# Copying the carries of two states in one GpSimd operation, with four scan buffers, a ring of two channel pairs for dt*x, and a new table of places

## What is computed

```python
x, z = split(hidden @ in_proj_w.T)                  # 1024 channels each
x = silu(causal_conv(x, conv_w, taps=4) + conv_b)
dt, Bm, Cm = split(x @ x_proj_w.T)                  # 64, 16, 16 columns
dt = softplus(dt @ dt_proj_w.T + dt_proj_b)
A = -exp(A_log)                                     # 1024 x 16
h = exp(dt * A) * h + dt * Bm * x                   # step by step over the tokens
y = (sum over the 16 states of h * Cm) + x * D
y = (y * silu(z)) @ out_proj_w.T
x = layernorm(hidden + y)
x = layernorm(x + relu(x @ Wq1.T + b1) @ Wq2.T + b2)   # Wq: weights quantised to -1, 0, 1
```

## Time and profile before

| | |
|---|---|
| median of 3 runs | 4741.44 us (4734.76 to 4742.01) |
| the profiled execution | 4733.51 us, its span 4731.7 us |
| busy over the span: PE, DVE, ACT, POOL | 93%, 83%, 72%, 67% |
| first scan of chunks 7 and 8 of 16 (the middle chunk read below) | at 1429.6 and 1656.8 us |
| last gate of the state-space part | begins at 3706.88 us (two gates) |

### The profile page before, as it was taken

The page is one execution under the profiler, slowest core; times in us unless marked ns, Lnnn a source line. Parts: engine busy times, 40 slices in busy tenths (PEclk is TensorE's granted clock), DMA queues, the critical chain, the costliest instruction groups (busy, mean ns, idle before and its releaser), DMA issues.

```text
span 4731.7 us, 85297 instructions
## 1 busy us (share of the span) xinstructions
PE 4423.0 (93%) x23362; PEld 3138.7 (66%) x23362; DVE 3941.4 (83%) x4785; ACT 3429.0 (72%) x6626; POOL 3162.0 (67%) x2462
## 2 busy tenths in 40 slices
PE   7999998999999898989898989899987899999998
PEld 4666666666666566656565666566655688888887
DVE  6999999999999898989898999899999644444444
ACT  5889898989898989888989888888987322222221
POOL 4797979898989888888888898989798200000000
PEclk8999999999999999999999999999999999999999
DMA  3333333333333333333333333333344100111101
GB/s 112 103 98 104 112 101 112 101 116 103 107 111 108 113 101 112 103 104 110 110 108 104 108 109 109 110 103 109 104 128 131 49 36 28 34 35 35 35 35 36
DMA packets 233417, 436.66 MB, mean 92 GB/s; under 512 B 24016, under 2 KB 24144, under 8 KB 232464
## 3 DMA queue, kind: packets, MB, share of 16 engines
q1 hardware_dynamic: 232976, 431.55, 29.1%
...
## 4 chain that ended last, share of the span: by engine, by line
POOL 33%; PE 27%; issue 19%; ACT 12%; DVE 8%; POOLq 1%; ACTq 0%; DVEq 0%; DMA 0%; SPq 0%
POOL dbu L649 26%; PE ht L1442 9%; PE y L1455 5%; PE gemm L1455 5%; DVE h L978 4%; ACT ch L717 4%; ACT decay L703 3%; PE gemm L1233 3%; PE ht L1285 2%; POOL x L586 2%; PE y L1290 2%; POOL carry L626 2%; POOL dtx L599 2%; POOLq L54 1%; POOL soft L591 1%
## 5 line engine op out<-in xcount | busy, mean ns | idle before, releaser
L978 DVE TENSOR_TENSOR_SCAN h<-decay,carry,dbu 128x512 f32<-128x512 f32 x2048 | 2526.5, 1269 | 189.2 <-ACT decay L703 124.9
L649 POOL TENSOR_TENSOR dbu<-dtx,bb 128x1024 f32<-128x1024 f32 x1024 | 2442.4, 2385 | 59.9 <-DVE dtx L1078 52.6
L703 ACT ACTIVATE decay<-dt,aneg 128x512 f32<-128x512 f32 x2048 | 1439.6, 705 | 264.7 <-DVE h L978 257.5
L1285 PE MATMUL ht<-ident,h 128*128 128x128 f32 x8192 | 1263.3, 284 | 256.9 <-ACT ch L717 178.4
L717 ACT ACTIVATE ch<-ht,ct 128x256 f32<-128x256 f32 x3328 | 1405.6, 484 | 123.6 <-PE ht L1285 123.1
L1285 PEld LDWEIGHTS ht<-ident,h 128*128 128x128 f32 x8192 | 970.6, 145 | 781.5 <-ACT ch L717 379.1
L1233 PE MATMUL gemm<-xt,win 128*128 128x512 f32 x1984 | 975.0, 600 | 17.0 <-ACT z L769 14.3
L1290 PEld LDWEIGHTS y<-ident,ch 128*128 128x128 f32 x6656 | 789.0, 144 | 243.8 <-issue 226.5
L1290 PE MATMUL y<-ident,ch 128*128 128x128 f32 x6656 | 894.0, 278 | 2.4 <-DVE x L1005 2.0
L898 ACT ACTIVATE hr<-ht,b1c 128x512 f32<-128x512 f32 x256 | 176.3, 689 | 753.0 <-PE ht L1442 753.0
L626 POOL TENSOR_TENSOR carry<-h,ones_pair 128x2 f32<-128x2 f32 x1022 | 289.9, 284 | 470.1 <-DVE h L978 454.3
...
## 6 DMA issues: line engine op xcount, KB each, us to landing
bb<-b_rows SPq DMA_DIRECT2D x1024, 256.0 KB, 3.5
win<-w_in SPq DMA_DIRECT2D x256, 256.0 KB, 2.7
...
```

The lines of the kernel that those rows point to most:

```text
L649: nc.gpsimd.tensor_tensor(dbu[:, u % 2, :, :], dtx[:, pair(q), :], bb[:, u % BB_RING:u % BB_RING + 1, :].to_broadcast([P, 2, TC]), ALU.mul ...
L703: nc.scalar.activation(DA[j][:, :], dt[:, c.par, i, :], ACT.Exp, scale=aneg[:, i, n:n + 1])\
L978: nc.vector.tensor_tensor_scan(h[:, H_SLOT[u], j, :], DA[j][:, :], dbu[:, u % 2, j, :], carry[:, c.par, n, i:i + 1], ALU.mult, ALU.add).th ...
L1285: ins = nc.tensor.transpose(HT[k][:, tb % 2, j * P:(j + 1) * P], h[:, H_SLOT[u], j, tb * P:(tb + 1) * P], ident[:, :])
```

## The change

It does the following:

- `save_state` becomes `save_states`: at an odd unit u it copies the carries of units u-3 and u-2 with one operation of 2x2 values for a partition; `ones_pair` gets that shape. It waits for the scans of unit u-2. The semaphore `carried` now counts pairs (`CARRIES` = 32 a chunk), and those who wait for it are changed to match.
- h gets four buffers, used in turn, so that units u and u+1 with even u lie side by side.
- dtx shrinks from 8 blocks to a ring of two channel pairs. `make_dtx` waits until the products of the pair two before are made.
- `BY_DVE` goes from 12 units to 14: 9 and 54 leave it, 2, 7, 52 and 58 join.
- All tables of places have new numbers.
- In the feed-forward part xhi lies in the memory of z (it was in that of dtx), and its first writer waits for four gates.

Its core:

```diff
-BY_DVE = (1, 3, 9, 12, 17, 38, 39, 45, 47, 54, 57, 60)
+BY_DVE = (1, 2, 3, 7, 12, 17, 38, 39, 45, 47, 52, 57, 58, 60)
-H_SLOT = [u % 3 for u in range(UNITS - 4)] + [1, 0, 2, 1]
+H_RING = 4
+H_SLOT = [u % H_RING for u in range(UNITS)]
+CARRIES = UNITS // 2
...
-EXP_AT = {9: 2, 11: 3, 97: 0, 103: 1}
-LN_AT = {14: (2,), 22: (3,), 106: (0,), 108: (1,)}
+EXP_AT = {5: 2, 9: 3, 97: 0, 102: 1}
+LN_AT = {15: (2,), 21: (3,), 105: (0,), 108: (1,)}
...
-ADD_AT = {8: 1, 15: 3, 34: 9, 43: 12, 59: 17, 121: 38, 124: 39, 141: 45, 146: 47, 169: 54, 179: 57, 185: 60}
+ADD_AT = {10: 1, 11: 2, 16: 3, 26: 7, 43: 12, 58: 17, 121: 38, 122: 39, 141: 45, 148: 47, 163: 52, 176: 57, 180: 58,
+          186: 60}
...
-ROUND_AT = {17: (2,), 21: (3,), 151: (0,), 161: (1,)}
-LIFT_AT = {20: (2,), 24: (3,), 157: (0,), 159: (1,)}
-DT_SUM_AT = {47: 2, 50: 3, 165: 0, 176: 1}
-SKIP_AT = {7: ((3, 0),), 8: ((3, 1),), 56: ((0, 0),), 57: ((0, 1),), 104: ((1, 0), (1, 1)), 149: ((2, 0), (2, 1))}
+ROUND_AT = {21: (2,), 23: (3,), 152: (0,), 161: (1,)}
+LIFT_AT = {17: (2,), 23: (3,), 155: (0,), 157: (1,)}
+DT_SUM_AT = {38: 2, 54: 3, 165: 0, 175: 1}
+SKIP_AT = {8: ((3, 0),), 9: ((3, 1),), 56: ((0, 0),), 58: ((0, 1),), 105: ((1, 0), (1, 1)), 149: ((2, 0),),
+           150: ((2, 1),)}
...
-EXCESS_AT = {12: 2, 15: 3, 55: 0, 56: 1}
-DTX_AT = {3: (2,), 9: (3,), 20: (4,), 28: (5,), 29: (6,), 33: (7,), 57: (0,), 59: (1,)}
-GATE_AT = {3: (6,), 4: (7,), 60: (0, 1), 61: (2, 3), 62: (4,), 63: (5,)}
-CORR_AT, FIX_AT = 6, 38
+EXCESS_AT = {10: 2, 15: 3, 55: 0, 58: 1}
+DTX_AT = {5: (2, 3), 21: (4,), 28: (5,), 33: (6,), 40: (7,), 56: (0,), 58: (1,)}
+GATE_AT = {3: (6,), 4: (7,), 60: (0, 1, 2), 61: (3,), 62: (4,), 63: (5,)}
+CORR_AT, FIX_AT = 2, 40
...
-                wait(pool, dbu_ready, f, UNITS, (i // 2 - NP + 1) * NS)
+                wait(pool, dbu_ready, f, UNITS, (i // 2 - 1) * NS)
...
-            def save_state(c, u):
+            def save_states(c, u):
                 q, n = u // NS, u % NS
-                wait(pool, scanned, c, SCANS, 2 * u + 2)
-                nc.gpsimd.tensor_tensor(carry[:, c.par, n, pair(q)], h[:, H_SLOT[u], :, TC - 1], ones[:, :], ALU.mult)\
-                    .then_inc(carried, 1)
+                wait(pool, scanned, c, SCANS, 2 * u + 4)
+                nc.gpsimd.tensor_tensor(carry[:, c.par, n:n + 2, pair(q)], h[:, H_SLOT[u]:H_SLOT[u] + 2, :, TC - 1],
+                                        ones[:, :, :], ALU.mult).then_inc(carried, 1)
...
-                    if u >= 2:
-                        save_state(c, u - 2)
-                    elif not is_first:
-                        save_state(p, UNITS - 2 + u)
+                    if u % 2 and u >= 3:
+                        save_states(c, u - 3)
+                    elif u == 1 and not is_first:
+                        save_states(p, UNITS - 2)
```

90 lines of the change are left out of this document (44 added, 46 removed), and 9 rows, old and new, of tables (CONV_AT, OUT_AT).

## The result

The changed kernel takes 4796.74 us (median of 4 runs, 4791.14 to 4804.43) against 4740.48 us of the kernel before in the same job (4 runs, 4734.76 to 4742.01). The ratio is 1.0126, with a 95% interval of 1.0114 to 1.0138: 56 us slower, where 14 us faster was forecast, and above the range. The profiled execution is the slowest of the four: 4804.43 us, with a span of 4802.6 us, 70.9 us above that of the earlier trace rows.

The account below looks back on a forecast made before the run. VectorE was taken to bound units 0-39 of a chunk, ScalarE 40-53, GpSimd the rest. Terms 1.6 - 0.5 - 0.5 - 0.9 - 0.6 = -0.9 us a chunk, over 15 chunks -13.5 us, gave 4727 us; range 4692 to 4765.

Parts of the forecast that it names:

- Loads: only their units move: Loads on SP's queue: their counts stay and only their units move; no time was counted.
- Carries: Units 54 to 63: 12 carries become 6, taking 0.9 us a chunk off GpSimd's bound; between -1.0 and -0.6.
- The prediction's own signs of being wrong: Profile after: GpSimd gaps in the last stretch, dt sums and lifts over 1.6 us, or ya's transpose waits above 3 us.
- shared port: Rival: moved VectorE lifts and sums meet GpSimd products midway, eight a chunk, +84 us, 4825 us; 3%.
- The handover at unit 52: Slow carry of 1.26 us ahead of unit 54's product goes, last stretch begins earlier: -0.6 us a chunk, 0 to -1.3.
- Two units: BY_DVE from 12 to 14: one added in units 0 to 39 costs VectorE +1.6 us a chunk, one in units 54 to 63 nothing.
- The head: Start of a chunk: both skips one scan later, so VectorE waits less for TensorE: -0.5 us a chunk, up to +0.5.
- units 8 and 9: GpSimd is late here and scans wait for its product; four fewer carries in eight units give -0.5 us, 0 to -1.0.
- Four buffers and the ring: Four scan buffers and the dt*x ring of two channel pairs: no added wait, counted as nothing.
- GpSimd bounds the last stretch: Units 54 to 63 with the next chunk's first products: GpSimd busy 44.81 of 44.9 us, so only its savings shorten it.
- VectorE's stretch grows: Rival: pair 1's excess after unit 58's product makes VectorE late for unit 59; only +1.6 us remains, +24 us, 4765; 16%.
- twin sum: In the rival of VectorE's growing stretch: a second dt sum, at unit 58, waiting for an excess like unit 55's 1.16 us.

Follow-up runs that it names:

- e13: Changed kernel plus 64 increments of an unread semaphore on TensorE, once, ahead of all chunks: 4770.09 us, ratio 1.0069.
- e9: Changed kernel with both 1 MB loads put back (xt at unit 16, xres at unit 1): 4775.98 us, ratio 1.0079.
- e17: Changed kernel with e9's loads, e10's spare GpSimd operation and e13's 64 increments: 4760.84 us, ratio 1.004.
- e10: Changed kernel plus a spare small GpSimd multiplication at every even unit: 4786.06 us, ratio 1.0098.
- e15: Kernel before plus the same 64 semaphore increments on TensorE: 4737.81 us, ratio 0.9999.
- e3: Kernel before with only the xt load moved to unit 2: 4739.5 us, ratio 0.9999.
- e6: Kernel before with only the xres load moved to unit 5: 4739.3 us, ratio 1.0002.
- e4: Changed code (pair carries, four buffers, ring) with the BY_DVE and places of before, save dt*x of block 6 at unit 33: 4812.18 us, ratio 1.0151.
- e7: e4 with 64 single carries a chunk in place of pairs, four buffers and ring kept: 4738.93 us, ratio 0.9999.
- e8: e4 with its pair carries, plus a spare two-value GpSimd product where the single carry is missing: 4736.56 us, ratio 0.9995.
- e12: Changed kernel with e9's loads and e10's spare operation, units 2 and 58 taken off BY_DVE (12 units): 4780.58 us, ratio 1.0086.
- e16: Kernel before with the excess of pair 1 made by VectorE, not GpSimd, just ahead of its dt sum: 4762.93 us, ratio 1.0055.
- e18: Changed kernel's places and 14 units, but 64 single carries, with e9's loads and e13's increments: 4762.37 us, ratio 1.005.

## Why the prediction was wrong

**"Loads: only their units move", counted as nothing.** This, and the lack of any term for the loop's edge, is the largest miss. Odd heads and unit 63 hold 56 of the 70 us; beside even heads at 14, the stall behind the edge is some 29, or 19 to 23 against a usual execution of the kernel before, and unit 63 13. That much of it is not a matter of the order of work is shown: 64 unused instructions take 27 us away (e13), the loads' places 21 (e9), both together hardly more (25 us, e17 against e10). The time of the kernel before doesn't answer to the padding (e15) or to either load alone (e3, e6). That the missing thing is code is argued from e13 and from waits on nothing right behind a jump, not shown by itself; why the kernel before loses so much less at the same jumps stayed open.

**Carries, "6 x 0.15 = 0.9 us come off the bound".** The price of a carry was right: 32 a chunk, some 0.20 us each where nothing blocks them. But the step counted only a carry's own time, and not that it stands between a wait and a long product and so decides who gets the port. In the old places this costs 72 us (e4, e7, e8), in the new ones 16 us at units 40 to 62 against 6 to 8 us gained in the rest (e10). One carry of 0.2 us that was missing at the wrong place cost the dt sum 2.1 us; in e4 three of the 32 a chunk made such a loss, by its rows. The prediction's own signs of being wrong came true here: a mean of the dt sums over 1.6 us (1870 ns), and gaps of GpSimd in the last stretch.

**The rival "shared port", at 3%.** Its mechanism was the right one, its trigger wrong: it was argued from where the VectorE operations stand, right behind a unit's second scan, and that speaks for a collision once GpSimd has no small operation there. With the code alone its price was near (72 us against 84 forecast), by luck: it counted eight lifts and sums at 0.7 us each, and three operations were hit by 2.1 to 2.2 us each, one of them a round, a kind that it had left out. The new places avoid most of it: the lifts got faster (1217 ns), and only the dt sum of unit 55 is hit, 2.1 us a chunk. What would have told it was already printed: the order of GpSimd's instructions from unit 54 on, where a carry stands between the excess and the next product before and none does now, read beside the earlier trace rows.

**The handover at unit 52, -0.6.** The lifts did get faster and the slow carry went: the product of unit 54 waits for the scans and for no carry. But the second stretch, which had to end sooner for the gain to count, is only 0.1 us shorter in this chunk.

**Two units, +1.6 in the first stretch.** The first stretch is longer by 0.5 us, as summed, but not by this term: e12 took a unit out of its head and the head stayed at 22.1 us. In that head GpSimd is as full as VectorE (21.22 and 21.49 of 21.50 us), with the correction and a dt*x moved into it; the forecast read VectorE's 134.29 of 135.7 us as the only bound. The hit is by chance. What a unit spares TensorE was also misnamed: the transposes into HT are as many as before (8192), and the additions into Y fell from 6656 to 6400.

**The head, -0.5, and units 8 and 9, -0.5.** The waits of scans for products fell by 19.0 us over the run, 1.2 a chunk; that was right and more. The waits of the skips rose instead, to 34.8 us, 27.9 of them behind the edge (6.9 before).

**Four buffers and the ring, nothing.** Right: e7 is at 0.9999 of before.

**"GpSimd bounds the last stretch".** True of its busy time, and the sum made of it was false: taking 2.35 us off GpSimd, at the price of 1.64 on VectorE, made it 24 us slower overall (e16). **The rival "VectorE's stretch grows"** gave a last stretch that is no shorter, which happened, but its place was wrong: the trouble is at unit 55, not 58, and its twin sum is not the cause (1.86 us in the changed kernel, 1.91 before).

What stays open: 22 to 24 us that the loads, the padding and the carries don't explain (e17, e18). By the table they are heads and units 6 to 39 together (+16 to 19 us), unit 63 (+8 to 10) and units 40 to 62 (+3 to 4). Some 6 to 10 of the odd heads' share is the short reference execution. No single instruction was found for the rest. The second theory of e18, that the places hold it, stands; the pairing is excluded. A rival that no run tests is TensorE's granted clock. Its mean over the profiled execution is 0.976 before, 0.964 in the changed kernel, 0.968 in e17 and 0.971 in e18, and at the low level TensorE's rows are slower (in the changed kernel eight additions into Y took 1.91 us at 1693.39, 1.04 at 1636.96 with the clock at its upper level). In the head behind the edge it is partly an effect of the pause: 0.83 in the changed kernel, 0.93 in e13 (chunk 7). What it costs in the last units is not known.
